# Attended values of two heads in one column group of TensorE: two transposes a batch instead of four, 256 columns copied instead of 512

## What is computed

```python
Q = split(layernorm(x) @ Wq); K = split(ctx @ Wk); V = split(ctx @ Wv)      # (8, 16, 128, 8)
scores = einsum('bhqd,bhkd->bhqk', Q, K) / sqrt(8)                          # layer 0: zero scores masked; layer 1: a mask
attn = softmax(scores, axis=-1)
out = einsum('bhqk,bhkd->bhqd', attn, V).transpose(0, 2, 1, 3).reshape(8, 128, 128)
x = x + out @ Wo (+ bo)
```

## Time and profile before

| | us |
|---|---|
| median of three runs | 656.22 |
| lowest and highest of the three | 652.84 and 657.77 |
| the profiled execution | 651.94 |
| its span, first to last instruction | 650.2 |

### The profile page before, as it was taken

How to read it: one execution, slowest core, us unless ns; L and a number is a source line. 1 busy time by engine, 2 the same in 40 slices (tenths; PEclk the granted TensorE clock), 3 DMA queues, 4 the chain that set the end, 5 groups by cost and what they waited for, 6 DMA issues and landing times.

```text
span 650.2 us, 17700 instructions
## 1 busy us (share of the span) xinstructions
PE 574.2 (88%) x7075; PEld 375.2 (58%) x7075; DVE 435.5 (67%) x1201; ACT 300.2 (46%) x520; POOL 210.5 (32%) x329
## 2 busy tenths in 40 slices
PE   8799975799999978798998988898899899899893
PEld 6477732487466643456765564675466476466452
DVE  6688588775455378876747746676776776776771
ACT  3244420111444417425555663555486486475572
POOL 7418440311420030052026735202530530530563
PEclk9999986899999999899999999999899999999997
DMA  6690045003300000000001127002231231231220
GB/s 152 162 326 13 3 133 159 21 14 110 150 2 2 2 1 1 1 1 3 2 2 50 47 65 249 2 2 68 67 93 43 67 93 43 72 89 42 68 52 18
DMA packets 45330, 40.42 MB, mean 62 GB/s; under 512 B 13139, under 2 KB 36727, under 8 KB 45120
## 3 DMA queue, kind: packets, MB, share of 16 engines
q1 hardware_dynamic: 40320, 29.87, 15.1%
q0 software_dynamic: 3584, 8.76, 5.5%
q10 hardware_dynamic: 1344, 0.66, 0.4%
HBM read 30.71 MB, written 8.81 MB: 61 GB/s over the span
## 4 chain that ended last, share of the span: by engine, by line
PE 71%; DVE 15%; issue 5%; ACT 4%; DMA 3%; POOL 1%; ACTq 0%; DVEq 0%; POOLq 0%
PE psum L2083 8%; PE psum L2057 7%; PE psum L669 7%; PE psum L679 6%; PE psum L2067 5%; PE psum L730 5%; PE psum L646 3%; PE psum L588 3%; PE psum L740 2%; PE psum L982 2%; PE psum L1501 2%; DVE scr L1175 2%; PE psum L749 1%; DMA scr<-y_d,rowi 1%; PE psum L685 1%
## 5 line engine op out<-in xcount | busy, mean ns | idle before, releaser
L396 ACT ACTIVATE scr<-psum 128x1024 f32<-128x1024 f32 x64 | 65.5, 1024 | 97.6 <-PE psum L679 36.6
L1618 ACT ACTIVATE b1r<-big 128x512 f32 x160 | 87.9, 620 | 33.8 <-DVE be L1824 27.5
L512 DVE TENSOR_REDUCE Mp<-psum 128x8 f32<-128x1024 f32 x64 | 77.8, 1220 | 20.6 <-PE psum L691 10.0
L669 PE MATMUL psum<-scr 32*128 32x256 f32 x512 | 72.1, 400 | 9.5 <-ACT scr L396 4.0
L368 POOL TENSOR_TENSOR scr<-KT,hmask 128x256 f32<-128x256 f32 x64 | 37.5, 612 | 128.8 <-DVE scr L1420 42.3
L679 PE MATMUL psum<-Qa,scr 32*128 32x128 f32 x1024 | 74.5, 283 | 0.0
L588 PE MATMUL psum<-fill,identb 128*128 128x512 bf16 x242 | 64.0, 405 | 0.0
L679 PEld LDWEIGHTS psum<-Qa,scr 32*128 32x128 f32 x1024 | 62.1, 186 | 1.9 <-issue 1.1
L669 PEld LDWEIGHTS psum<-scr 32*128 32x128 f32 x512 | 45.1, 184 | 28.4 <-issue 16.9
L1977 DVE COPY scr<-psum 128x512 f32<-128x512 f32 x48 | 33.2, 692 | 37.7 <-PE psum L2067 37.5
L2067 PEld LDWEIGHTS psum<-ident,scr 128*128 128x128 f32 x232 | 24.6, 142 | 47.4 <-issue 25.9
(11 more groups left out here) (416 smaller groups left out, 1211.3 us busy)
## 6 DMA issues: line engine op xcount, KB each, us to landing
y_d<-scr SPq DMA_DIRECT2D x36, 130.0 KB
big<-in_L_ffn_W SPq DMA_DIRECT2D x2, 2048.0 KB, 10.1
big<-in_L_ffn_W SPq DMA_DIRECT2D x8, 512.0 KB, 9.3
big<-in_L_ffn_W SPq DMA_DIRECT2D x1, 4096.0 KB, 13.7
b1r<-in_L_ffn_b SPq DMA_DIRECT2D x1, 2048.0 KB, 11.0
scr<-y_d,rowi POOLq DMA_INDIRECT x36, 3.6
b2r<-in_L_ffn_b SPq DMA_DIRECT2D x1, 512.0 KB, 12.8
xn_d<-xn SPq DMA_DIRECT2D x1, 512.0 KB, 3.6
```

The costliest lines, as they stand in the source:

```text
L396: act.activation(PT[i % 2][:, c, :], pair(WU), ACT.Exp, scale=SCALE).then_inc(S(f"exp{c}"), 1)
L512: dve.tensor_reduce(Mpe[:, :, :, :, c, DH], pair(2 * c).rearrange("p (r b j k) -> p r b j k", r=2, b=2, j=2), AX.X, ALU.max, negate=True). ...
L669: ins = pe.matmul(bank[2 * e + r][:, 2 * P * c:2 * P * c + 2 * P], QT[rows, c, i, :], Km[rows, i % KB, c, :, :].rearrange("p v k -> p (v k)"),
L1618: ins = act.activation(W2d[d % len(W2d)][:, F * u:F * u + F], W2[k.layer][:, bass.ds(e * F, F)], ACT.Copy)
```

## The change

Two heads now share one column group. The values of a pair lie side by side with nine zeros between: `Va` holds for each pair three fields of nine columns (head v = 0, zeros, head v = 1). A matmul takes 18 neighbouring columns of it as weights: the first head's nine and the zeros, or the zeros and the second head's nine. The two matmuls of a pair write to the same 18 rows of bank 6, the second adding to the first, so the first nine rows are one head's and the next nine the other's. The number of matmuls stays at 16 a batch. Their results take two blocks of 128 columns instead of four, so `copy_oU` copies 256 columns, `turn_outputs` turns two blocks, and reciprocal and division read them from there. GpSimd also clears the middle field once. `o_sb` becomes a part of `xs`, and `e8w` a part of `hs`, whose other uses come later.

```diff
-        Va = sb("Va", [P, B, H, DH + 1])
+        Va = sb("Va", [P, B, HC, 3, DH + 1])
-        o_sb = sb("o_sb", [P, D])
-        e8w = sb("e8w", [E8, 3, D])
+        e8w = hs[0:E8, 0:3 * D].rearrange("p (n d) -> p n d", n=3)
+        o_sb = xs[:, 0, :]
...
-                act.activation(oU[:, :], bank[6], ACT.Copy).then_inc(S("oU_copied"), 1)
+                act.activation(oU[:, 0:2 * P], bank[6][:, 0:2 * P], ACT.Copy).then_inc(S("oU_copied"), 1)
...
-                src = bank[2 + n].rearrange("p (b h d) -> p b h d", b=4, h=H)
-                dst = Va[:, 4 * n:4 * n + 4, :, 0:DH]
+                src = bank[2 + n].rearrange("p (b m v d) -> p b m v d", b=4, m=HC, v=2)
+                dst = Va[:, 4 * n:4 * n + 4, :, 0:3:2, 0:DH]
...
-                    last = dve.tensor_copy(dst, src)
+                    last = dve.tensor_copy(dst.rearrange("p b m v d -> p (b m) v d"), src.rearrange("p b m v d -> p (b m) v d"))
...
-                avs = turned(i).rearrange("p (h n) -> p h n", h=H)
-                link(dve, dve.reciprocal(rs[:, :].unsqueeze(2), avs[:, :, DH:DH + 1]))
-                dve.tensor_tensor(o_sb[:, :].rearrange("p (h d) -> p h d", h=H), avs[:, :, 0:DH],
-                                  rs[:, :].unsqueeze(2).to_broadcast([P, H, DH]), ALU.mult
+                avs = turned(i)[:, 0:2 * P].rearrange("p (m x) -> p m x", m=HC)[:, :, 0:2 * (DH + 1)
+                                                                             ].rearrange("p m (v n) -> p m v n", v=2)
+                two = rs[:, :].rearrange("p (m v) -> p m v", v=2).unsqueeze(3)
+                link(dve, dve.reciprocal(two, avs[:, :, :, DH:DH + 1]))
+                dve.tensor_tensor(o_sb[:, :].rearrange("p (m v d) -> p m v d", m=HC, v=2), avs[:, :, :, 0:DH],
+                                  two.to_broadcast([P, HC, 2, DH]), ALU.mult
...
-                for j in range(HC):
-                    r, b, v = j // 4, j // 2 % 2, j % 2
-                    h = HC * b + 4 * r + 2 * c + v
-                    p, g = 32 * (2 * r + v), 2 * c + b
-                    ins = pe.matmul(bank[6][p:p + DH + 1, P * g:P * g + P], Va[:, i, h, :],
-                                    PT[i % 2][:, c, P * j:P * j + P], start=True, stop=True)
+                for v in range(2):
+                    for b in range(2):
+                        for r in range(2):
+                            m, p, j = HV * b + 2 * r + c, 32 * (2 * b + r), 4 * r + 2 * b + v
+                            pair = Va[:, i, m, :, :].rearrange("p t n -> p (t n)")[:, (DH + 1) * v:(DH + 1) * (v + 2)]
+                            ins = pe.matmul(bank[6][p:p + 2 * (DH + 1), P * c:P * c + P], pair, PT[i % 2][:, c, P * j:P * j + P],
+                                            start=v == 0, stop=v == 1, skip_group_check=True)
...
-                for g in range(4):
+                for g in range(2):
                     ins = pe.transpose(turned(i)[:, P * g:P * g + P], oU[:, P * g:P * g + P], ident[:, :])
...
-            pool.memset(Va[:, :, :, DH:DH + 1], 1.0)
+            pool.memset(Va[:, :, :, 1, :], 0.0)
+            for v in (0, 2):
+                pool.memset(Va[:, :, :, v, DH:DH + 1], 1.0)
```

More of the change, by code:

```diff
@@ L481, in dve_values @@
                         last = dve.tensor_tensor(dst[:, b], src[:, b],
-                                                 bv[:, VB[L], :].rearrange("p (h d) -> p h d", h=H), ALU.add)
+                                                 bv[:, VB[L], :].rearrange("p (m v d) -> p m v d", m=HC, v=2), ALU.add)
                 else:
-                    last = dve.tensor_copy(dst, src)
+                    last = dve.tensor_copy(dst.rearrange("p b m v d -> p (b m) v d"), src.rearrange("p b m v d -> p (b m) v d"))
             last.then_inc(S("v_copied"), 1)
```

## The result

The changed kernel took 650.66 us in the median (649.27 to 653.63), the kernel before 654.45 (652.54 to 657.77), 13 runs of each side by side. The ratio is 0.9941 with a 95% interval of 0.9923 to 0.9959, so 3.8 us less, between 2.7 and 5.0. Later, on another occasion, the same kernel gave 0.9965 (0.9944 to 0.9986), 2.3 us less, between 0.9 and 3.7. The forecast was 3.4 us less. (Ratios here are those on record for all runs of both kernels; they need not be the quotient of the two medians.) As a time, the forecast of 652.8 lay 2.1 us too high, because it started from a median of three runs, 656.22, and the median of 13 was 654.45.

A forecast was written before the change was run, and what follows sets the result against it. The prediction took TensorE, busy 88% of the 650.2 us span, as the bound where it is itself late. Gains of 2.1 us in the loops and 1.3 at layer ends made 3.4, from 656.22 to 652.8 us; range 648.0 to 656.5.

The forecast's parts named there:

- Third and fourth layer, 0.11 kept in each of four batches: Batches 2 to 5: 0.11 us gained each before the exponential is late, 0.44 us in each layer.
- First layer, 0.01: Five first-layer batches: the exponential arrives with the last transpose, so slack is 0.01 us each, 0.05 in all.
- Second layer, 0.20: Four second-layer batches: the shifted queries (L494) come last, leaving 0.20 us slack each, 0.80 us together.
- Batch 6, 0.36: Batch 6 of the last three layers: fewer waits, half of 0.23 us each, 0.36 together, bounds 0 and 0.69.
- Ends of the layers, 1.3: Last turnings after the loops: 0.4 us each in layers one and four, 0.23 each in two and three, 1.3 together.
- Copy, 0: ScalarE's copy at L403 of 256 columns for 512: 0.597 us becomes about 0.387, counted 0, upper bound 0.8 us.
- 18 columns, 0: Attended values (L730): wider weight loads stay hidden behind matmuls of other column groups, 0, at most 0.3 us in all.
- GpSimd, up to 1.5 us, hidden: Clearing the padding at the start: up to 1.5 us more on GpSimd, hidden as its keys are read later, 0.
- VectorE and the moved buffers, 0: Values, reciprocal and division keep their element counts; two buffers move to places used later, with no wait added: 0.
- All of it counts: Rival: every nanosecond cut from the turning (L740) is gained, 7.5 us, ending at 648.7 us; chance 0.15.
- Nothing is released earlier: Rival: the loops give 0 and only the layer ends pay, 0.9 us, ending at 655.3 us; chance 0.10.
- Loads in the open: Rival: the 1,024 wider loads of attended values (L730) cost 7.6 us, net +4.2, ending at 660.4 us; chance 0.05.

The follow-up runs named there:

- the wait moved last: The changed kernel with TensorE's wait for the second exponential written last ahead of the phase's first matmul: 649.17 us, ratio to before 0.9931.
- the kernel before with the wait last: The kernel before with TensorE's wait for the second exponential written last ahead of the phase's first matmul: 653.31 us, ratio to before 0.9996.
- pairs together: The changed kernel with the two matmuls of a pair of heads issued one right after the other: 653.48 us (0.9975), again 652.08 us (0.9965).
- the waits split: The changed kernel with TensorE's waits for shifted queries and second exponential moved behind the first two scoring matmuls: 646.79 us (0.9872), again 646.85 us (0.9881).

## Why the prediction was right, point by point

*Two transposes fewer end 0.23 sooner.* Right: 0.41 for 0.63 on the chain.

*Third and fourth layer, 0.11 kept in each of four batches.* The mechanism is shown by the wait moved last, which gives back 0.11 more. The size was a little high: 5.02 to 4.93 us, about 0.09 a batch, 0.36 and 0.35 in a layer instead of 0.44. The way from the load of the scores to the end of the next exponential, which I took as fixed, came out at 4.70 us for 4.68, so 0.02 of the 0.11 went there.

*First layer, 0.01.* Right: 6.83 to 6.82. The profile before also holds one late batch there (7.05 us, absent in two later runs with four transposes), which makes its 43.10 look worse by 0.2; one in the third layer (5.08) adds 0.06.

*Second layer, 0.20.* Slightly low, from a row that I misread. The batches went from 6.73 to 6.51, the whole 0.22, 0.89 for the four instead of 0.80. The first batch of the earlier trace rows, which I took to wait for L494, waited for the exponential, of which the earlier trace rows has no line:

```profile
184.56 1.03 ACT L396 ACTIVATE scr<-psum 128x1024 f32<-128x1024 f32 x1 [0.99 <-PE psum L685]
```

It ended at 184.56 + 1.03 = 185.59, and the load at 185.81 is 0.22 later, the way of the earlier trace rows. So 0.16 was no least way from L494. The same batch of the kernel before with the wait last is 0.10 shorter, and there L494 is the last to be waited for:

```profile
184.75 0.42 DVE L494 TENSOR_TENSOR Qa<-psum,scr 128x256 f32<-128x256 f32 x1 [2.07 <-PE psum L719]
...
185.24 0.22 PEld L670 LDWEIGHTS psum<-scr 32*128 32x128 f32 x2 [0.34 <-issue]
```

The load begins 0.07 after its end. With that as the least way the slack is nearer 0.3 than 0.20, more than two transposes take, so nothing is lost. In a batch in the middle, after, the load begins 0.13 after the end of L494 and 0.17 after the last load of the turning, which is still the last:

```profile
200.79 0.42 DVE L494 TENSOR_TENSOR Qa<-psum,scr 128x256 f32<-128x256 f32 x1
...
200.97 0.20 PEld L743 LDWEIGHTS psum<-ident,hb 128*128 128x128 f32 x2 [0.46 <-issue]
...
201.34 0.19 PEld L671 LDWEIGHTS psum<-scr 32*128 32x128 f32 x2 [0.17 <-issue]
```

*Batch 6, 0.36.* Low: the step from the sixth turning on shrank by 0.11, 0.05, 0.22 and 0.22 us, 0.60 together. In the third and fourth layers that step is 4.79 us with the wait moved, too, so the exponential is not last there; all of the turning counts, and I had halved it.

*Ends of the layers, 1.3.* High. In the changed kernel the chain leaves TensorE after the last turning but one in the first three layers, not in two:

```profile
77.94 0.38 PE psum L743 x2
78.33 0.02 issue
78.35 0.27 DVE rs L502
...
333.92 0.38 PE psum L743 x2
334.31 0.02 issue
334.33 0.27 DVE rs L502
...
444.40 0.38 PE psum L743 x2
...
446.40 0.22 PE psum L743 x2
```

So one turning each in three layers and two in the fourth, where the chain holds both, at 0.22 by these pieces: 1.1. With the loops (0.36 + 0.35 + 0.03 + 0.89 + 0.60 = 2.2) that makes 3.3. The forecast was 3.4, from terms that were off by 0.1 to 0.2 each in both directions; that they cancel so nearly is luck.

*Copy, 0.* Right; its only visible 0.22 us is off the chain.

*18 columns, 0.* Right: loads of 97 ns on the mean, runs of 1.00 us, as the row of L2083 had it. The rule of the Trainium skill ("TensorE: Matmul & The Clock Gate", section "Part 3: Packing small matmuls — row/col tiling") that loads overlap only with matmuls of another row group does not hold here: all of these use 128 rows, and loads of 90, 97 and 105 ns on the mean, for 9, 18 and 27 columns, give runs of 1.00, 1.00 and 1.01 us. The same section also lets a load into the background weight buffer go ahead of running matmuls; these runs would fit that, but none of them shows the buffer. My own reason, that the column groups alternate, did not hold either: without the alternation the runs are 1.02.

*GpSimd, up to 1.5 us, hidden.* Right. The memsets took 0.97 us for 0.33, so 0.64 more and less than half of the bound, since 576 elements cost less than twice what 128 did (0.33 us):

```profile
12.06 0.61 POOL L2385 MEMSET Va<- 128x576 f32 x1
12.60 0.36 POOL L2387 MEMSET Va<- 128x64 f32 x2
```

From the first scores of the first layer to its first turning, the stretch behind them, it is 21.66 us before and 21.66 to 21.67 with 27 columns and in both runs of pairs together, all at a clock of 1.00: nothing of the memsets shows. (In the others with two transposes the clock there was 0.92, or waits had moved.)

*VectorE and the moved buffers, 0.* Right as far as seen: reciprocal and division take 252 and 292 ns on the mean, as before, and the run with four transposes, which keeps all of this, has the time of before.

*The rivals.* "All of it counts" fell because of the exponential and the order of waits; even with the waits split, the first layer's batches keep 0.13 of the 0.23 (6.83 to 6.70). "Nothing is released earlier" fell with the 0.22 to 0.23 seen in every steady batch of the first, third and fourth layers. "Loads in the open" fell with the 27 columns.

## What to carry to other kernels

Before counting a cut on the chain in full, take for each other thing that the next instruction waits for the time since it was ready, and subtract the least way from a batch where it really was last: that gives what the cut can bring before another wait takes its place. Make sure, too, which thing that batch waited for: another may have ended just as late, as in the earlier trace rows. Then look at the order in which the waits are written, and at their records in the trace: the one that comes true last belongs in the last stop, or behind the work that doesn't need it. And when the profile's clock differs between two executions, compare the stretches that hold the change, not the spans.

## What was not expected of the hardware

The 0.23 us from the end of a ScalarE instruction to TensorE's load were not one fixed latency: with the wait for it written last they were 0.11. Half of it was one further stop of TensorE's sequencer, for two other waits that had come true by then.

An attended-values matmul accumulating in the rows that the matmul just before it writes costs no more than 0.02 us in a run of 32 records.

Stretches without any of the change's work differed by 2 us at the same instructions, at a granted clock of 0.96 or 1.00. I have not found what decides which execution gets which; whether the change has a part in it stays open. It is not the change alone: from the last turning of the third layer to the first scores of the fourth, the kernel before took 62.2 us at 1.00, and the same kernel with its wait written last 64.0 us at 0.95.
